# Scales of a hidden FFN row: root and reciprocal root from one GpSimd operation, which also makes the dequantisation factor

## The reference, cut to what matters

```
def _rmsnorm(x, g):                      # EPS = 1e-08
    return g * (x * rsqrt(mean(x * x, axis=-1) + EPS))
def _act_quant(x):
    scale = 127.0 / clip(max(abs(x), axis=-1), 0.0001, None)
    return clip(round(x * scale), -128, 127) / scale
def _ternary_quant(w):
    s = mean(abs(w));  return round(tanh(w / (s + EPS))) * arctanh(s)
def _linear_bit(x, w, g):
    return einsum('bsd,od->bso', _act_quant(_rmsnorm(x, g)), _ternary_quant(w))
x = x + tanh(g_xattn[0]) * ssm(ctx_1024, layernorm(x), ...)     # scan over 512 steps, 512 channels x 16 states
xn = layernorm(x)                                               # 4 x 512 rows of 512
h = silu(_linear_bit(xn, w1, g1)) * _linear_bit(xn, w2, g2)     # rows of H = 2048: the hidden rows
x = x + tanh(g_ffn[0]) * _linear_bit(h, w3, g3)
```

## Time and profile before

| | |
|---|---|
| time, median of 3 runs | 740.04 us (739.11 to 740.69) |
| span of the profiled execution | 737.0 us |
| difference of the two | 3.0 us |
| DVE busy | 635.7 us, 86% of the span |
| PE busy | 629.0 us, 85% |
| ACT busy | 591.9 us, 80% |
| POOL busy | 559.0 us, 76% |
| mean granted clock of PE | 0.904 |

### The profile page before, as it was taken

One profiled execution on the slowest core, in us unless ns is written; L12 is line 12 of the kernel. 1 busy time (PEld: TensorE's weight loads), 2 busy tenths in 40 slices (PEclk: granted clock), 3 DMA queues, 4 the chain that ended last, 5 costly groups with the idle time before them and its releaser, 6 DMA issues.

```text
span 737.0 us, 8444 instructions
## 1 busy us (share of the span) xinstructions
PE 629.0 (85%) x2558; PEld 249.8 (34%) x2558; DVE 635.7 (86%) x725; ACT 591.9 (80%) x902; POOL 559.0 (76%) x309
## 2 busy tenths in 40 slices
PE   6555766988678999899989999989897979797997
PEld 3121221534234333334333433333332323233443
DVE  1579979899767999998999999999999999977675
ACT  4577875778678999988989999998797989667873
POOL 2026559787759899988989999898899898976731
PEclk9855876999797999999999999999797979798999
DMA  4299881455952112214421211144121111000000
GB/s 109 68 259 289 294 285 36 126 175 155 309 139 85 30 45 56 63 50 107 104 55 44 54 47 51 50 111 107 44 58 43 44 43 44 15 15 0 16 29 30
DMA packets 38461, 67.85 MB, mean 92 GB/s; under 512 B 10848, under 2 KB 13408, under 8 KB 36240
## 3 DMA queue, kind: packets, MB, share of 16 engines
q1 hardware_dynamic: 38416, 67.31, 31.8%
HBM read 46.32 MB, written 4.46 MB: 69 GB/s over the span
## 4 chain that ended last, share of the span: by engine, by line
DVE 49%; PE 21%; issue 11%; ACT 6%; POOL 6%; DMA 3%; SPq 1%; DVEq 0%; ACTq 0%; POOLq 0%
DVE hb L1132 25%; DVE dbu_ps L1123 13%; PE ring L1568 6%; POOL hb L637 3%; PE y_ps L1546 3%; PE ring L1654 2%; ACT dA L865 2%; DVE h_max L1282 2%; PE du_ps L1533 2%; DVE am L1192 2%; PE ring L1514 2%; PE ring L1495 2%; DMA bc_rep<-bc_scratch 1%; DVE u L1078 1%; PE ring L1471 1%
## 5 line engine op out<-in xcount | busy, mean ns | idle before, releaser
L1132 DVE TENSOR_TENSOR_SCAN hb<-dA,dbu_ps 128x1024 f32<-128x1024 f32 x128 | 292.4, 2284 | 12.9 <-ACT dA L865 3.7
L637 POOL TENSOR_TENSOR hb<-hb,bc_rep 128x2048 f32<-128x2048 f32 x52 | 235.9, 4536 | 63.5 <-DVE hb L1132 52.3
L865 ACT ACTIVATE dA<-dl_rep,a_neg 128x511 f32<-128x511 f32 x252 | 160.8, 712 | 20.0 <-DMA dl_rep<-delta 15.0
L1123 DVE TENSOR_TENSOR dbu_ps<-du_ps,bc_rep 128x1024 f32<-128x1024 f32 x128 | 157.7, 1232 | 17.5 <-PE du_ps L1533 11.3
L1533 PE MATMUL du_ps<-du,sel_q 32*128 32x512 f32 x128 | 82.9, 731 | 52.4 <-DVE dbu_ps L1123 52.4
L1546 PE MATMUL y_ps<-hb,sel_s 128*32 128x512 f32 x512 | 125.5, 636 | 1.7 <-POOL hb L637 1.7
L614 POOL TENSOR_TENSOR h<-h,up_sb 128x1024 f32<-128x1024 f32 x24 | 56.5, 2355 | 16.1 <-ACT up_sb L883 15.7
L1654 PE MATMUL ring<-w3T,hT 128*128 128x512 fp8e4 x256 | 59.8, 379 | 1.5 <-ACT hT L951 1.0
L632 POOL TENSOR_TENSOR hb<-hb,bc_rep 128x1024 f32<-128x1024 f32 x22 | 51.8, 2356 | 8.6 <-DVE hb L1132 8.3
L1546 PEld LDWEIGHTS y_ps<-hb,sel_s 128*32 128x32 f32 x512 | 28.5, 116 | 87.0 <-issue 82.2
L1568 PE MATMUL ring<-w1T,a12T 128*128 128x512 fp8e4 x208 | 54.8, 387 | 2.3 <-DVE x L1261 1.2
(11 more groups left out here) (182 smaller groups left out, 1048.9 us busy)
## 6 DMA issues: line engine op xcount, KB each, us to landing
dl_rep<-delta SPq DMA_DIRECT2D x252, 64.0 KB, 2.0
bc_rep<-bc_scratch SPq DMA_DIRECT2D x32, 256.0 KB, 4.7
h<-in_L_ffn_w_dram SPq DMA_DIRECT2D x8, 1024.0 KB, 7.8
x<-in_L_ffn_w_dram SPq DMA_DIRECT2D x8, 1024.0 KB, 6.6
up_sb<-in_L_ffn_w_dram SPq DMA_DIRECT2D x8, 1024.0 KB, 7.1
xt<-in_x_dram SPq DMA_DIRECT2D x16, 256.0 KB, 3.6
out_dram<-x SPq DMA_DIRECT2D x16, 256.0 KB, 2.1
x<-in_x_dram SPq DMA_DIRECT2D x2, 1024.0 KB, 6.3
```

Source lines behind the costliest of these rows:

```text
L637: g.tensor_tensor(hb[:, s % 4, :, :], hb[:, s % 4, :, :], c_rep(s // 16), ALU.mult)\
L865: ins = a.activation(dA[:, s % 2, i, 1:L], dl[:, 1:L], ACT.Exp, scale=a_neg[:, s % 16, i:i + 1])
L1123: v.tensor_tensor(dbu_ps[:, :, :], du_ps[:, :].unsqueeze(1).to_broadcast([P, 2, L]), b_rep(b)[:, 2 * half:2 * half + 2, :], ALU.mult).then ...
L1132: v.tensor_tensor_scan(hb[:, s % 4, 2 * half:2 * half + 2, :].rearrange("p a l -> p (a l)"), dA[:, s % 2, 2 * half:2 * half + 2, :].rearra ...
```

## The change

DVE no longer adds the squares, makes the mean or the dequantisation factor, and makes the scales in three instructions. POOL adds the two sums and H * EPS itself (hidden_rms), and raises the total in one instruction, broadcast to two columns, to 0.5 and to -0.5 (h_pow). The scale of the row as it is quantised is then the reciprocal of max(1e-4 / sqrt(H) * root, M1, M2) / 127, in which the row's norm cancels; POOL multiplies the factor of the way down by the reciprocal root (hidden_deq), and sqrt(H) goes once into alpha. Where POOL waited for h_ms it now waits for hss_done, and output waits for POOL's h_deq_done.

```
@@ pool
+            link(g.memset(halves[:, 0:1], 0.5))
+            link(g.memset(halves[:, 1:2], -0.5))
-            def hidden_rstd(ft):
-                pool.wait_ge(h_ms, ft + 1)
-                g.tensor_tensor(h_sc[:, 1:2], h_sc[:, 0:1], half_neg[:, :], ALU.pow).then_inc(h_rstd, 1)
+            def hidden_rms(ft):
+                pool.wait_ge(hss_done, 2 * (ft + 1))
+                link(g.tensor_scalar(h_ss[:, 2:3], h_ss[:, 0:1], h_ss[:, 1:2], H * RMS_EPS, ALU.add, ALU.add))
+                pool.wait_ge(h_scale, ft)
+                g.tensor_tensor(h_pow[:, :], h_ss[:, 2:3].to_broadcast([P, 2]), halves[:, :], ALU.pow).then_inc(h_rstd, 1)
+            def hidden_deq(ft):
+                pool.wait_ge(h_scale, ft + 1)
+                pool.wait_ge(o_done, ft)
+                pool.wait_ge(h_rstd, ft + 1)
+                if ft == 0:
+                    pool.wait_ge(alpha_done, 1)
+                g.tensor_scalar(h_deq[:, :], h_sc[:, 1:2], h_pow[:, 1:2], alpha[:, 2:3], ALU.mult, ALU.mult)\
+                 .then_inc(h_deq_done, 1)
@@ pool, blocks and tail
-                            hidden_rstd(gt)
+                            hidden_rms(gt)
...
                             mul_gains(f)
+                        if gt >= 0:
+                            hidden_deq(gt)
...
                 h_gain(ft, 0)
+                hidden_deq(ft - 1)
                 if ft < NT - 1:
                     h_gain(ft, 1)
-                hidden_rstd(ft)
+                hidden_rms(ft)
+            hidden_deq(NT - 1)
@@ scalar, square_sum
-                    act.wait_ge(h_ms, ft)
+                    act.wait_ge(h_rstd, ft)
@@ vector, alpha
-                link(v.tensor_tensor(alpha[:, 2:3], alpha[:, 2:3], gates[:, 1:2], ALU.mult))
+                v.tensor_scalar(alpha[:, 2:3], alpha[:, 2:3], gates[:, 1:2], float(np.sqrt(H)), ALU.mult, ALU.mult)\
+                 .then_inc(alpha_done, 1)
@@ vector, output
+                dve.wait_ge(h_deq_done, ft + 1)
@@ vector (square_total, mean_square and hidden_deq are gone, and their calls)
             def hidden_scales(ft):
-                link(v.tensor_scalar(h_sc[:, 2:3], h_max[:, 0:1], h_max[:, 1:2], None, ALU.max))
                 dve.wait_ge(h_rstd, ft + 1)
-                link(v.tensor_scalar(h_sc[:, 3:4], h_sc[:, 2:3], h_sc[:, 1:2], 1e-4, ALU.mult, ALU.max))
-                link(v.reciprocal(h_sc[:, 5:6], h_sc[:, 3:4]))
-                v.tensor_scalar(h_sc[:, 4:5], h_sc[:, 5:6], h_sc[:, 1:2], 127.0, ALU.mult, ALU.mult)\
-                 .then_inc(h_scale, 1)
+                link(v.tensor_scalar(h_sc[:, 0:1], h_pow[:, 0:1], float(1e-4 / np.sqrt(H)), h_max[:, 0:1], ALU.mult, ALU.max))
+                link(v.tensor_scalar(h_sc[:, 1:2], h_sc[:, 0:1], h_max[:, 1:2], 1.0 / 127.0, ALU.max, ALU.mult))
+                v.reciprocal(h_sc[:, 2:3], h_sc[:, 1:2]).then_inc(h_scale, 1)
```

More of the change, by code:

```diff
@@ L196, in flamingo_block @@
         h_max = sb("h_max", [P, 2])
-        h_sc = sb("h_sc", [P, 6])
+        h_pow = sb("h_pow", [P, 2])
+        halves = sb("halves", [P, 2])
+        h_sc = sb("h_sc", [P, 3])
         h_deq = sb("h_deq", [P, 1])
@@ L284, in flamingo_block @@
         h_mul = sem("h_mul")
-        h_ms = sem("h_ms")
+        h_deq_done = sem("h_deq_done")
         h_rstd = sem("h_rstd")
+        alpha_done = sem("alpha_done")
         h_scale = sem("h_scale")
@@ L717, in _ @@
             row_rstd(TAIL + 3)
-            hidden_rstd(TAIL - 1)
+            hidden_rms(TAIL - 1)
             mul_gains(TAIL + 1)
@@ L921, in quant_hidden @@
                     half = gained(ft)[:, H // 2 * i:H // 2 * (i + 1)]
-                    a.activation(half, half, ACT.Copy, bias=QMAGIC, scale=h_sc[:, 4:5]).then_inc(h_quant, 1)
+                    a.activation(half, half, ACT.Copy, bias=QMAGIC, scale=h_sc[:, 2:3]).then_inc(h_quant, 1)
             def evac_aT(ft):
@@ L1295, in quant_last @@
                 dve.wait_ge(h_scale, NT)
-                v.tensor_scalar(half, half, h_sc[:, 4:5], QMAGIC, ALU.mult, ALU.add).then_inc(h_last, 1)
+                v.tensor_scalar(half, half, h_sc[:, 2:3], QMAGIC, ALU.mult, ALU.add).then_inc(h_last, 1)
             def hidden_scales(ft):
-                link(v.tensor_scalar(h_sc[:, 2:3], h_max[:, 0:1], h_max[:, 1:2], None, ALU.max))
                 dve.wait_ge(h_rstd, ft + 1)
-                link(v.tensor_scalar(h_sc[:, 3:4], h_sc[:, 2:3], h_sc[:, 1:2], 1e-4, ALU.mult, ALU.max))
-                link(v.reciprocal(h_sc[:, 5:6], h_sc[:, 3:4]))
-                v.tensor_scalar(h_sc[:, 4:5], h_sc[:, 5:6], h_sc[:, 1:2], 127.0, ALU.mult, ALU.mult)\
-                 .then_inc(h_scale, 1)
+                link(v.tensor_scalar(h_sc[:, 0:1], h_pow[:, 0:1], float(1e-4 / np.sqrt(H)), h_max[:, 0:1], ALU.mult, ALU.max))
+                link(v.tensor_scalar(h_sc[:, 1:2], h_sc[:, 0:1], h_max[:, 1:2], 1.0 / 127.0, ALU.max, ALU.mult))
+                v.reciprocal(h_sc[:, 2:3], h_sc[:, 1:2]).then_inc(h_scale, 1)
             def evac_hT(ft):
@@ L1349, in _ @@
                     if q == 1 and g >= 0:
-                        ss = square_total(g)
                         hidden_max(g, 0)
-                        after(ss)
-                        mean_square(g)
                         top = hidden_max(g, 1)
@@ L1402, in _ @@
                             dequant_scales(f)
-                        if g >= 0:
-                            hidden_deq(g)
             def rows(ft):
@@ L1414, in hidden_row_scales @@
                     hidden_max(ft, 0)
-                after(square_total(ft))
-                mean_square(ft)
                 after(hidden_max(ft, 1))
@@ L1445, in _ @@
                 hidden_max(ft, 0)
-                hidden_deq(ft - 1)
                 if ft < NT - 1:
@@ L1452, in _ @@
             evac_hT(NT - 1)
-            hidden_deq(NT - 1)
             output(NT - 1)
```

## The result

| | before | changed |
|---|---|---|
| time, median of 20 runs each | 742.21 us (738.51 to 747.91) | 738.15 us (733.83 to 742.75) |
| ratio | | 0.9936, 95% interval 0.9914 to 0.9958 |
| span of the profiled execution | 737.0 us | 737.1 us |
| first scan of block 5 starts at | 239.66 us | 244.58 us |
| from there to the start of the last output (M) | 494.10 us | 489.25 us |

The changed kernel is faster by 0.64% (0.42 to 0.86), 4.7 us by that ratio; forecast were 4.6. The two medians alone differ by 4.06. So the kernels are compared over M, the part that holds every hidden row: 4.85 us shorter in these two traces.

What follows compares the result with a forecast made beforehand. DVE's instruction list was taken to bound blocks with a hidden row, PE the tail. Gains of 4.2 (blocks 5 to 12), 0.1 (13 and 14) and 0.4 (tail), less 0.1, made 4.6: 740.04 to 735.4 us, range 733.4 to 738.2.

Steps and rivals of the forecast that it cites:

- the scales: DVE's four scale instructions, 0.82 us, become three at 0.58, saving 0.24 in an ordinary block.
- blocks 13 and 14: Late blocks said to save almost nothing, DVE waiting there for exps and h_gain; 0.1 us for the two.
- The factor: The dequantisation factor, hidden_deq, leaves DVE's list for POOL, saving 0.24 us in an ordinary block.
- square_total and mean_square: Two small instructions leave DVE's list, 0.18 us a block, buying nothing in blocks 5 and 7.
- The addition of 0.30 + 0.05 leaves 0.55: In front of mul_du, POOL's addition and wider power use part of 0.90 us of cover; 0.55 stays.
- Blocks 5 to 12: Eight blocks at 0.66 us, 5.3, less 0.6 in 5 and 7 and 0.5 in 8 and 12: 4.2.
- it is as long as the block: Blocks 13 and 14: the loop from gated_y through half-clock PE and ACT holds no removed instruction and equals the block.
- Block 15 and tail: Block 15 gives nothing, POOL's power being late already; the tail, where PE is the bound, gives 0.4 us.
- dear POOL operations: Rival: POOL's power costs 1.10 us, its tensor_scalars 0.55, eating most gain; 739.0 us, chance 0.08.
- Cover gone: Rival: h_gain's second half leaves only 0.06, so 0.48 of 0.66 is lost in five blocks; 737.8 us, chance 0.10.
- The half-clock stretch moves: Rival: PE's half-clock stretch in blocks 12 to 15 falls elsewhere against its work; 733.5 or 738 us, chance 0.16.
- POOL becomes the bound: Rival: each new or changed POOL instruction costs 0.93 us, filling POOL's idle time; 742.5 to 746 us, chance 0.06.

Runs made afterwards that it cites:

- e_rms_early: Changed kernel with POOL's addition and power put ahead of times_c instead of behind it, some 4.5 us earlier; M 490.13 us, ratio 0.9953 to the kernel before.
- e_keep_before: Kernel before with 19 instead of 4 filler matmuls ahead of the gated_y transposes in blocks 12 to 15; M 492.64 us, ratio 0.9985 to the unedited kernel before.
- e_keep_after: Changed kernel with 19 instead of 4 filler matmuls ahead of the gated_y transposes in blocks 12 to 15; M 486.93 us, ratio 0.9936 to the kernel before.
- e_dear_front: Changed kernel with POOL's two-column power done twice, with a wait between; M 492.62 us, ratio 1.0000 to the kernel before.
- e_dear_deq: Changed kernel with POOL's dequantisation product done four times, each waiting for the one before; M 494.30 us, ratio 1.0020 to the kernel before.
- e_deq_dve: Changed kernel with the dequantisation factor made on DVE again, where it stood before; M 492.29 us, ratio 0.9969 to the kernel before.
- after_again: Changed kernel unaltered, traced once more in one run; M 489.53 us.
- e_sum_dve: Changed kernel with the sums of squares and H * EPS added on DVE in one instruction; M 488.83 us, ratio 0.9935 to the kernel before.
- e_scales4: Changed kernel with four dependent scale instructions on DVE again, maximum and division by 127 apart; M 492.12 us, ratio 0.9945 to the kernel before.
- before_again: Kernel before unaltered, traced once more in one run; M 495.81 us.

## Why the prediction was right

The time, 4.6 forecast and 4.7 measured (3.1 to 6.4 by the interval), and the mechanism hold: DVE's list was the block in most places, and an instruction taken from it shortened the block wherever no input was just in time. Of the terms two were off, the scales and blocks 13 and 14, by 0.5 and 0.7 us, and cancelled: that the sum came out so close is luck. The 735.4 us stood on the 740.04 of three runs, where twenty gave 742.21. And the prediction's own sign, an ordinary block shorter by 0.66, is there in block 10 alone (0.69); the other three, 6, 9 and 11, gave 0.35, 0.44 and 0.54.

- *The factor*, 0.24 a block: 0.25 in each of eleven blocks, 14 and 15 included.
- *square_total and mean_square*, 0.18: 0.18 in blocks 6 and 8 to 13, nothing in 5 and 7, where hidden_max waits for h_gain. Right in each.
- *The scales*, 0.24: nothing in 8 and 12, as forecast, and nothing in 5 and 7 either, where 0.11 was forecast. But also almost nothing in 9, and half in 11 and 13. Two steps were mis-sized. One is "The addition of 0.30 + 0.05 leaves 0.55", here in block 9, where POOL's power ends at 416.34 and DVE starts at 416.45, 0.10 us later than its list would have it.

```profile
415.25 0.29 POOL L624 TENSOR_SCALAR h_ss<-h_ss 128x1 f32<-128x1 f32 x1
415.62 0.72 POOL L626 TENSOR_TENSOR h_pow<-h_ss,halves 128x2 f32<-128x2 f32 x1
416.51 1.27 POOL L585 TENSOR_TENSOR delta<-delta,relu 128x512 f32<-128x512 f32 x1 [0.17 <-DVE delta L1124]
```

```profile
416.45 0.21 DVE L1312 TENSOR_SCALAR h_sc<-h_pow,h_max 128x1 f32<-128x1 f32 x1
```

  Of the 0.90 of cover, addition and wider power take 0.54 (0.37 from start to start, and 0.72 less 0.55), not 0.35, and hidden_deq, which POOL meets in the same round, up to 0.34 more; and from the power's end to DVE's start pass 0.11. The prediction charged hidden_deq to the exps alone, though it stands in the one list that also leads to the next power. In blocks 13 and 14 this is the whole loss: with the power early (e_rms_early) the scales get it back.

  The other step is the cover behind ACT. The prediction subtracted z_stats in blocks 5 and 7 alone. In block 9 z_stats ends 0.31 later against the scans, by hidden_deq, and holds z_var whatever the power does; in block 11 ACT's part of log1p holds DVE (e_rms_early above).
- *Blocks 5 to 12* together: 4.2 forecast, 3.6 measured (3.58 by the table). The scales gave 0.67 of the 1.2 counted on; the two entries "else", -0.35 and 0.18, are stalls that nobody had forecast.
- *Blocks 13 and 14*: 0.1 forecast, 0.81 measured. The step that failed is "it is as long as the block": the loop through PE at half clock ended where DVE needed it, to 0.03 and 0.21 us, and was read as a second bound. e_keep_before shows that it bound next to nothing there (full clock, 0.01 and 0.08 gained). The loop starts at DVE's gated_y, which comes earlier when DVE does, and the producers on it had themselves been waiting. In blocks 14 and 15 of the changed kernel it does bind, by 0.5 and 0.9 (e_keep_after), and shows as these waits:

```profile
602.70 0.21 DVE L1312 TENSOR_SCALAR h_sc<-h_pow,h_max 128x1 f32<-128x1 f32 x1 [0.18 <-POOL h_pow L626]
...
634.54 1.22 DVE L1293 TENSOR_REDUCE h_max<-up_sb 128x1 f32<-128x1024 f32 x1 [0.31 <-POOL up_sb L612]
```

- *Block 15 and tail*: 0.4 forecast, 0.45 measured; the steps between the tail's rows gave 0.06 to 0.09 each, as forecast, and 0.25 for the last. It is the sum of a loss and a gain: block 15's scans come 0.48 later than they would, and the tail takes that back, since it waits for PE.

Of the rivals, *dear POOL operations* had the sizes wrong (0.715 for the power, not 1.10; 0.30 to 0.34, not 0.55), but e_dear_front shows its price was real: 0.78 more takes 2.5 of M's 4.85 us, without the stretch at 385 us, and leaves no gain in the runs' times that could be told from none. *Cover gone* came true in part, at the power and behind ACT, and not at h_gain in ordinary blocks. *The half-clock stretch moves*: it does, by execution more than by the change. *POOL becomes the bound* would have needed more than 1.3 us more at one place: e_dear_deq reaches 1.0020 (0.9997 to 1.0044).

The Trainium skill (GPSIMD Engine Reference, § 4.1 Engine selection), which spoke against the move, gives its factor of about two for operations with two inputs and calls those with one roughly as fast as on VectorE. The product, with one tensor and two per-partition factors, takes 0.34 on POOL against 0.26 on DVE in e_deq_dve, but only 0.18 of DVE's list, so about twice in what it costs an engine. The price doesn't decide here, because POOL had the time and DVE had not.

## What to carry over

When one engine's list is the block, price each removed instruction from start to start, and then subtract, place by place, what the receiving engine adds ahead of each result that the first one takes, summed over its whole list since it last waited and not only over what stands beside that result, and what a third engine behind it adds in turn. An input that arrives just in time is a second bound only if its producer wasn't itself waiting for the engine in question; the chain has to be followed back once round the loop. And where single runs scatter by 1%, intervals between the same two instructions of two traces still agree to 0.01 us, away from PE's half-clock stretches, and can carry terms that no total can.

## What was not expected of the hardware

- A power over two columns costs 0.715 us against 0.55 for one, and a tensor_scalar with per-partition operands 0.30 to 0.34 on POOL, where a three-column product takes 0.20.
- DVE's stalls of about 0.35 us go with its program and not with the time. In block 6 of the changed kernel add_input starts 0.46 after the scan (usually 0.1) with nothing late:

```profile
289.39 1.23 DVE L1145 TENSOR_TENSOR dbu_ps<-du_ps,bc_rep 128x1024 f32<-128x1024 f32 x1 [0.46 <-DVE hb L1154]
```

  The same instruction is late by the same 0.35 to 0.37 in after_again, e_rms_early, e_keep_after, e_dear_front and e_dear_deq, whose DVE programs are alike. With one instruction more in each block it stands elsewhere: one interval between scans earlier in e_deq_dve, in block 12 in e_sum_dve, in block 10 and at the first scan of 13 in e_scales4. Before had a smaller one, 0.22, in block 12 (at 534.57), and so have before_again and e_keep_before. In all twelve traces one packet of the DMA queue of kind "instruction", q14, starts 0.65 to 0.92 us behind the late instruction: here it is the only packet of any queue between 289 and 291 us, at 290.08.

```profile
q14 instruction: 1, 0.01, 1.3%
```

  The queue has packets behind no stall too, and the traces don't say for which engine one is. That DVE's program is loaded there is likely, then, and not shown: no run tested it.
- PE fell to half clock (1.2 GHz) around its idle 3.5 to 4.8 us in blocks 12 to 15, in each trace of both kernels, and near 387 us in before_again, at a cost of 2.3 us over two blocks, but not in the first trace of the same kernel. Its longest idle times ahead of that place were 1.02 and 0.79 us, and 1.04 and 0.77 in the trace that kept full clock. The Trainium skill (TensorE: Matmul & The Clock Gate, Part 1) says that where a kernel meets the change varies from run to run; this second stretch, 0.84 and 0.82 in the two windows above against 1.00 in the first trace, agrees.
